# Int16 sums in seven buffers, differences on VectorE and a later load of the node rows in a two-layer graph kernel

## What is computed

```python
xn = _layernorm(x)
out = xn @ root + bias
for r in range(8):
    mask = (edge_type == r)
    sums = segment_sum(xn[src] * mask[:, None], dst, 625)
    cnt = segment_sum(mask, dst, 625)
    out = out + (sums / max(cnt, 1)[:, None]) @ weight[r]
```

## Time and profile before

| | us |
|---|---|
| median of 3 runs | 2971.97 |
| lowest and highest | 2968.42 and 2972.78 |
| the profiled execution | 2970.98 |
| its span, first to last instruction | 2969.2 |
| tallies, first to last matmul | 1832.77 to 2035.31 |
| start of the first sums of relation 0 | 2054.69 |

### The profile page before, as it was taken

The page is one execution under the profiler, slowest core; times in us unless marked ns, Lnnn a source line. Parts: engine busy times, 40 slices in busy tenths (PEclk is TensorE's granted clock), DMA queues, the critical chain, the costliest instruction groups (busy, mean ns, idle before and its releaser), DMA issues.

```text
span 2969.2 us, 39308 instructions
## 1 busy us (share of the span) xinstructions
PE 2723.3 (92%) x15859; PEld 2364.4 (80%) x15859; DVE 1805.1 (61%) x2019; ACT 1309.2 (44%) x1669; POOL 527.2 (18%) x475
## 2 busy tenths in 40 slices
PE   5989988999999999999679996789999999999988
PEld 5967778777777767776569995468999999999987
DVE  6467654778787887787635555676444444444443
ACT  3225422666766766766256665563111111112221
POOL 5776405431230000000100000343000000000000
PEclk8999999999999999999889998799999999999989
DMA  5224016999998999999441113676222221132212
GB/s 147 68 74 121 1 57 191 317 327 323 326 332 321 334 323 328 330 320 325 155 167 43 43 40 103 217 255 223 79 79 79 72 72 50 50 120 77 74 55 70
DMA packets 151178, 496.61 MB, mean 167 GB/s; under 512 B 25419, under 2 KB 38091, under 8 KB 149986
## 3 DMA queue, kind: packets, MB, share of 16 engines
q1 hardware_dynamic: 116482, 429.41, 41.4%
q0 software_dynamic: 19424, 41.25, 4.9%
q10 hardware_dynamic: 15092, 23.44, 2.5%
HBM read 422.70 MB, written 71.13 MB: 166 GB/s over the span
## 4 chain that ended last, share of the span: by engine, by line
PE 74%; DVE 10%; DMA 7%; ACT 3%; POOL 3%; issue 2%; SPq 0%; ACTq 0%; DVEq 0%; POOLq 0%
PE ps L195 73%; DMA er<-in_wd 3%; POOL lc L1419 2%; DVE es_l L220 2%; DVE T_l L220 2%; ACT es_h L682 1%; DMA scr_tl<-T_l 1%; DMA scr_adj<-acc 1%; DMA wr<-in_Wk 1%; DVE acc L216 1%; DVE x L208 0%; PE ps L1747 0%; ACT ws_h L682 0%; DVE ws_l L220 0%; PE ps L1059 0%
## 5 line engine op out<-in xcount | busy, mean ns | idle before, releaser
L220 DVE TENSOR_TENSOR es_l<-er,es_h 128x1408 fp32r<-128x1408 f32 (+1 forms) x455 | 654.1, 1446 | 196.6 <-ACT es_h L682 192.9
L682 ACT ACTIVATE es_h<-er 128x1408 fp32r<-128x1408 f32 (+1 forms) x455 | 563.8, 1242 | 260.6 <-PE ps L195 179.3
L195 PE MATMUL ps<-T_h,ws_h 128*128 128x314 f32 x1856 | 431.2, 314 | 22.1 <-DVE T_l L220 13.8
L682 ACT ACTIVATE ws_h<-wr 128x1024 fp32r<-128x1024 f32 (+1 forms) x181 | 190.8, 1054 | 553.4 <-PE ps L195 502.6
L195 PE MATMUL ps<-T_h,ws_l 128*128 128x314 f32 x1856 | 421.5, 308 | 0.0
L195 PE MATMUL ps<-T_l,ws_h 128*128 128x314 f32 x1856 | 420.7, 308 | 0.0
L195 PEld LDWEIGHTS ps<-T_h,ws_h 128*128 128x128 f32 x1856 | 311.4, 191 | 30.7 <-DVE T_l L220 16.1
L195 PEld LDWEIGHTS ps<-T_h,ws_l 128*128 128x128 f32 x1856 | 312.5, 191 | 0.0
L195 PEld LDWEIGHTS ps<-T_l,ws_h 128*128 128x128 f32 x1856 | 312.5, 190 | 0.0
L220 DVE TENSOR_TENSOR ws_l<-wr,ws_h 128x1024 fp32r<-128x1024 f32 x173 | 210.1, 1216 | 129.8 <-ACT ws_h L682 128.0
L195 PE MATMUL ps<-es_h,xe_h 128*98 128x512 f32 (+1 forms) x768 | 208.4, 379 | 10.3 <-DVE es_l L220 6.9
(11 more groups left out here) (427 smaller groups left out, 5083.7 us busy)
## 6 DMA issues: line engine op xcount, KB each, us to landing
er<-in_wg SPq DMA_DIRECT2D x128, 704.0 KB, 6.8
er<-in_wu SPq DMA_DIRECT2D x128, 704.0 KB, 5.9
er<-in_wd SPq DMA_DIRECT2D x176, 512.0 KB, 5.1
scr_adj<-acc SPq DMA_DIRECT2D x123, 314.0 KB, 2.9
wr<-in_rel SPq DMA_DIRECT2D x64, 512.0 KB, 3.5
wr<-in_Wqkv SPq DMA_DIRECT2D x24, 512.0 KB, 3.5
steps<-scr_adj POOLq DMA_DIRECT2D x7, 1570.0 KB, 8.1
wr<-in_gate SPq DMA_DIRECT2D x16, 512.0 KB, 3.5
```

What stands on the lines that cost most here:

```text
L195: return e.matmul(out, l, r, start=start, stop=stop, skip_group_check=True)
L220: return e.tensor_tensor(lo, src, hi.bitcast(F32), ALU.subtract)
L682: q.e.activation(c.hi, c.at, ACT.Copy).then_inc(*self.s("high").up(c.key))
```

## The change

- `acc`, `scr_adj` and `steps` are int16 instead of float32. `acc` has seven buffers, and `v_tally` of chunk c waits for the store of c-7. `steps` has two buffers.
- The rows by nodes are loaded by GpSimd (`p_back`): `nat_h` just before `blc` of chunk 64, `nat_l` just before that of chunk 72.
- VectorE takes the differences (`v_counts`): those of relation 0 block by block before `v_over` of relation 0, those of relation r+1 after the third `ua` of relation r. GpSimd only issues the loads (`p_steps`).

```diff
-        for i in range(4):
-            at(f"acc{i}", R3 + 20224 + i * 2528, NT)
+        for i in range(7):
+            at(f"acc{i}", R3 + 20224 + i * 1280, NT, I16)
...
-        at("steps", R3, T * NT)
+        for i in range(2):
+            at(f"steps{i}", R3 + i * 6304, T * NT, I16)
...
-        if c > 3:
-            q.wait_ge(self.landed(f"tally{c % 4}"), c - 4)
+        if c > 6:
+            q.wait_ge(self.landed(f"tally{c % 7}"), c - 7)
...
+            if c in (64, 72):
+                self.p_back(q, c == 72)
             e.tensor_scalar(m[f"blc{c % 5}"], self.iota[:, 0:128], seb[:, c, 0:1], None, ALU.is_equal).then_inc(*self.s("chunk_sources").up(c))
...
+    def p_back(self, q, i):
+        n, b = (("nh", "nat_h"), ("nl", "nat_l"))[i]
+        q.wait_ge(self.s("attention_sums"), ("out", 7, 1))
+        q.wait_ge(self.s("out_low"), 7)
+        q.wait_ge(self.landed("kept_norm"), 3)
+        for f, g in shares(TP):
+            q.e.dma_start(self.m[b][f:g, :].bitcast(F32), self.d[n][f:g, :]).then_inc(*self.landed("norm_by_nodes").up(i))
...
         for r in range(8):
+            if r == 0:
+                self.v_counts(q, 0)
             self.v_over(q, r)
...
+                if o == 2 and r < 7:
+                    self.v_counts(q, r + 1)
...
         for t in range(T):
-            e.dma_start(steps[:, t, :], self.d_adj[t * 128:(t + 1) * 128, :]).then_inc(*self.landed(f"steps{t}").up(0))
-        for t in range(T):
-            q.wait_ge(self.landed(f"steps{t}"), 0)
-            e.tensor_tensor(rows(self.counts(0), T)[:, t, 0:NT - 1], steps[:, t, 1:NT], steps[:, t, 0:NT - 1], ALU.subtract).then_inc(*self.s("counts").up((0, t), 0))
+            e.dma_start(rows(m["steps0"], T)[:, t, :], self.d_adj[t * 128:(t + 1) * 128, :]).then_inc(*self.landed(f"steps_of_block{t}").up(0))
         for r in range(1, 8):
-            q.wait_ge(self.s("counts"), r - 1)
+            if r > 1:
+                q.wait_ge(self.s("counts"), r - 2)
+            self.p_steps(q, r)
+
+    def v_counts(self, q, r):
+        m = self.m
+        steps, to = rows(m[f"steps{r % 2}"], T), rows(self.counts(r), T)
+        if r == 0:
+            self.all_stored(q)
+            for i in range(2):
+                q.e.memset(self.counts(i)[0:TP, NT - 1:T * NT:NT].bitcast(I32), 0)
+            for t in range(T):
+                q.wait_ge(self.landed(f"steps_of_block{t}"), 0)
+                tt(q.e, to[:, t, 0:NT - 1], steps[:, t, 1:NT], steps[:, t, 0:NT - 1], ALU.subtract).then_inc(*self.s("counts").up((0, t), 0))
+        else:
+            q.wait_ge(self.landed(f"steps{r % 2}"), r)
             if r > 1:
                 q.wait_ge(self.s("aggregated"), (("agg", r - 2), KD - 1))
+            tt(q.e, to[:, :, 0:NT - 1], steps[:, :, 1:NT], steps[:, :, 0:NT - 1], ALU.subtract).then_inc(*self.s("counts").up(r))
```

More of the change, by code:

```diff
@@ L11 @@
 U16 = mybir.dt.uint16
+I16 = mybir.dt.int16
 AX = mybir.AxisListType.X
@@ L189, in at @@
     def at(self, name, off, n, dt=F32):
-        assert off % 32 == 0 and off + n * (2 if dt in (BF16, U16) else 4) <= self.size, (name, off, n)
+        assert off % 32 == 0 and off + n * (2 if dt in (BF16, U16, I16) else 4) <= self.size, (name, off, n)
         return self.nc.alloc_sbuf_tensor_at(name, [128, n], dt, offset=self.base + off)[:, :]
@@ L2018, in v_tally @@
         m, ps = self.m, self.ps
-        acc, was = m[f"acc{c % 4}"], m[f"acc{(c - 1) % 4}"]
+        acc, was = m[f"acc{c % 7}"], m[f"acc{(c - 1) % 7}"]
         q.wait_ge(self.s("tallied"), c)
-        if c > 3:
-            q.wait_ge(self.landed(f"tally{c % 4}"), c - 4)
+        if c > 6:
+            q.wait_ge(self.landed(f"tally{c % 7}"), c - 7)
         for i, cut, src in self.tally_halves(c):
@@ L2081, in s_store_tallies @@
                 q.wait_ge(*self.ps.done(("tally", c), i))
-            e.dma_start(self.d_adj[bass.ds(v, 128), :], m[f"acc{c % 4}"]).then_inc(*self.landed(f"tally{c % 4}").up(c))
+            e.dma_start(self.d_adj[bass.ds(v, 128), :], m[f"acc{c % 7}"]).then_inc(*self.landed(f"tally{c % 7}").up(c))
     def t_attention(self, q):
@@ L2511, in v_mean @@
         else:
-            for i in range(4):
-                q.wait_ge(self.landed(f"tally{i}"), NCH - 1 - (NCH - 1 - i) % 4)
+            self.all_stored(q)
         tt(q.e, two(m[f"ta{k % 2}"]), ps.two(ps.group[("agg", r), k][0]), two(m["icnt"]), ALU.mult).then_inc(*ps.out((("agg", r), k)))
@@ L2577, in p_relations, with p_steps @@
             if r > 1:
                 q.wait_ge(self.s("aggregated"), (("agg", r - 2), KD - 1))
-            e.tensor_tensor(rows(self.counts(r), T)[:, :, 0:NT - 1], steps[:, :, 1:NT], steps[:, :, 0:NT - 1], ALU.subtract).then_inc(*self.s("counts").up(r))
+            tt(q.e, to[:, :, 0:NT - 1], steps[:, :, 1:NT], steps[:, :, 0:NT - 1], ALU.subtract).then_inc(*self.s("counts").up(r))
+    def p_steps(self, q, r):
+        q.e.dma_start(rows(self.m[f"steps{r % 2}"], T), self.d_adj[r * T * 128:(r + 1) * T * 128, :].rearrange("(s p) n -> p s n", p=128)).then_inc(*self.landed(f"steps{r % 2}").up(r))
@@ L2583, in t_gate, with all_stored @@
+    def all_stored(self, q):
+        for i in range(7):
+            q.wait_ge(self.landed(f"tally{i}"), NCH - 1 - (NCH - 1 - i) % 7)
     def t_gate(self, q):
```

6 lines of the change are left out of this document (2 added, 4 removed).

## The result

The changed kernel takes 2932.45 us (median of 4 runs, 2928.18 to 2935.85) where the kernel before took 2971.64 in the same comparison: a ratio of 0.9869, 95% interval 0.9852 to 0.9886. Two later comparisons of the same two kernels gave 0.9887 (0.9871 to 0.9904) and 0.9902 (0.9885 to 0.9918), so the gain is 29 to 39 us; the mean of the three ratios makes it 34. The prediction was 2935, within 2923 to 2951.

A forecast was written before the change was run, and what follows sets the result against it. The prediction took TensorE, busy 92% of the span, as the bound, with gains only where it stands, mainly behind late stores. Terms of 1.4+28.9-7+6.3+6.5=36.1 us off 2971 gave 2935 us, range 2923 to 2951.

The forecast's parts named there:

- Start: Before the first tally: ACT no longer issues four DMAs, so the first tally starts earlier; gain 1.4 us.
- Stalls on stores: Tallies, chunks 4 to 122: seven buffers and half the bytes remove VectorE's waits for stores; gain 28.9 us together.
- The rows by nodes: Tallies near chunks 66 and 74: the later bulk load stalls stores once, then near 0; loss 7 us, bounds 0 and 16.
- Rival A: Tallies: the bulk load stalls twice, a loss of 12 to 16 us for 7; 2940 to 2944 us; chance 0.17.
- Rival B: Tallies: no loss from the bulk load, as seven buffers or passing stores cover it; 2928 us; chance 0.12.
- After the last store: Between tally 122 and the first sums: differences on VectorE end with the root matmuls; gain 5.0, plus 1.3 slow clock.
- rival E: Stores wait for SP, which issues them between weight loads; half of the 28.9 us comes; 2949 us; chance 0.10.
- The relations: Relations: without GpSimd's difference beside it T_l no longer holds TensorE, six times 1.08 us; gain 6.5 us.
- C: Relations: T_l did not hold TensorE, or VectorE comes late; 6.5 shrinks to 4 or nothing; 2938 to 2942; chance 0.10.
- D: Tallies: int16 slows VectorE's tally, which then sets the pitch; 65 us of loss against 36 of gain; 3000 us; chance 0.04.
- the signs that I had named: Right if store waits fall under 8 us, tally 122 starts 20 to 26 us earlier, T_l takes 0.80 us throughout, among others.

The follow-up runs named there:

- its likes: Two runs with the kernel before unaltered up to tally 122: VectorE taking the differences, 2956.79 us; GpSimd's difference made to wait, 2957.01 us.
- the later difference: The kernel before, with GpSimd's difference for relations 1 to 7 waiting for the third block of the previous relation's product: 2957.01 us, ratio 0.9971.

## Why the prediction was right, and where it was not

The time was right, but as a sum whose two largest errors nearly cancelled: the load cost some 3 us more than I gave it, and the relations gained 2.7 more. Part of it is luck besides, since the profile that the stalls were read from had 4.5 us more of them than its likes.

*Start* (1.4): shown, 1.39, and given back when ScalarE issues the load again.

*Stalls on stores* (28.9): without the load the same stretches, 4 to 122, are 29.5 us shorter than in the profile of before, and 25 shorter than in its two likes. The sum took one profile's stalls as the kernel's, 4.5 us too many. The reason was half wrong too. I named seven buffers and half the bytes, and spoke of "nearly all that gets in its way" without saying what that is: apart from the load of the rows by nodes it is mostly the weight load on the same queue (17.0 of the 34.1 us), in which the bytes of a store have next to no part. Of int16 with four buffers I expected a loss of 5 to 12 us, and it was 24.

*The rows by nodes* (a loss of 7, between 0 and 16): 9.3 to 10.6. The mechanism held, one full stall and a second near nothing, but the first was mis-sized at "4 to 5 us" where VectorE waited 9.4. The step that failed is the length of a half, 9.5 to 10 us from 133 packets in 10 us, with the end of the crawl put 12 to 13 us behind tally 59. With a weight load and seven stores beside it the two DMAs of the half landed after 13.5 and 16.0 us, and the store issued with them after 15.9, which is 17.6 us behind tally 59. Rival A's 12 to 16 is off on the other side, and for the wrong reason: not two stalls, but one longer, though VectorE did wait a second time, 3.5 us at chunk 74. Rival B, no loss, is refuted for whole rows. The two queues in three stretches of that time, 1922 to 1927, 1927 to 1930 and, when the load had ended, 1935 to 1938 us (the first number counts the profile's packets):

```profile
q0 software_dynamic: 57, 1.17, 93.1%
```

```profile
q0 software_dynamic: 42, 0.86, 103.0%
q1 hardware_dynamic: 41, 0.05, 7.5%
```

```profile
q1 hardware_dynamic: 635, 1.00, 98.0%
q0 software_dynamic: 3, 0.00, 0.2%
```

For 5 us the stores, of which four were issued in that time, moved nothing at all. Then they moved one packet for one of the load's, but a packet of theirs has 1,256 bytes and one of the load's 20,480, so that a third of a store (41 of 128) passed in 3 us. Behind the load 635 went in 3 us. By the Trainium skill ("DMA: Bandwidth & Descriptors", Queues, rings and completion order) an engine drains a whole packet of one queue, some 9 to 17 descriptors, before it turns to the next. In the prediction I had taken that as help for the stores, and the trace of before as speaking against it. It would hold for the load's rows as well, of which an engine gets some 8 (125 over 16 engines), and the stores would stand behind all of them. The trace agrees for the first 5 us and not for the next 3, in which the two queues moved 42 and 41. No run here shows where a packet in the skill's sense ends, so that the rule behind this stays open.

*After the last store* (5.0, with 1.3 for the slow clock): 3.9. I had the differences and the root matmuls end together. They ended 2.2 us apart:

```profile
2011.79 1.03 SPq L664 DMA_DIRECT2D wr<-in_rel  x1
2013.39 2.24 SPq L2095 DMA_DIRECT2D scr_adj<-acc  x3
...
2019.96 2.80 POOL L2576 DMA_DIRECT2D steps<-scr_adj  x5 [11.34 <-DMA scr_adj<-acc]
...
2024.66 2.97 DVE L209 TENSOR_TENSOR A_h<-steps 128x627 fp32r<-128x627 int16 x4 [1.14 <-DMA steps<-scr_adj]
2025.51 0.79 ACT L2496 ACTIVATE ua<-ps,bcol 128x628 f32<-128x628 f32 x1 [6.35 <-PE ps L196]
```

SyncE put a relation's weights ahead of the last three stores, for 1.03 us, and issued the last at 2015.30, 1.4 us behind VectorE where I had 0.2; it landed in 3.8 us where I had 3.3, and the rest of the chain took about 0.2 us more than I gave it. This is rival E's mechanism, at one place and for 1 us.

*The relations* (6.5): 10.2, of which 1.0 is the slow clock at the first sums (the first period was 82.9 us, the next five 81.9), that I had booked with 1.3 at the step before. The rest, 9.2, is 6 x 1.5. I took TensorE's wait from the row of its matmuls, 1.08. The row of its weight loads stands beside it with 1.34 (in the fence above), so the matmuls' row did not hold all of it. A period before is 81.9 us and a period after 80.36: that difference, 1.5, was to be had from the trace of before. The last relation of before, beside which no difference runs, has 80.32.

The rivals C and D are refuted: T_l takes 0.80 us throughout and no wait of TensorE is left in the relations, and int16 costs nothing.

Of the signs that I had named, the time of tally 122 (22.7 us earlier), T_l and the tally's two forms came as said. VectorE's waits for stores did not: 12.9 us where I had under 8, and the second one ended 34 us behind the issue of `nat_h`, not within 25. Nor did the first sums, 2.6 us behind the end of the root matmuls where I had 2.

## What to carry to other kernels

How many buffers a stream of stores needs was set here by what stood ahead of a store or beside it in the queues, and hardly by the store's own bytes. The measure is the longest landing, against the time until a buffer is needed again: the number of buffers times the pitch, less the step that fills one and its issue (at the waits measured 1.7 to 3.2 us with four, 4.2 to 5.3 with five, 6.5 and over with seven). A bulk load beside such a stream should be cut up and spread until the longest landing is under that time; moving it whole only moved its stall. Whether the size of a piece, the length of its rows or the distance between pieces did it, these runs do not say. What a wait costs the engine that sets the pace is best taken as the difference of two periods with and without it, since each row of idle time sees only its part.

## What the runs showed of the hardware that I had not expected

The price of the collision: GpSimd's whole instruction. The longest T_l of the kernel before took 5.48 us for 0.80, and `ws_l` beside the later difference 5.48 for 1.21:

```profile
L220 DVE TENSOR_TENSOR T_l<-ta,T_h x58: 800/804/5476, 2079.9 to 2652.5; 128x628 fp32r<-128x628 f32 x58
```

The type of what is read costs VectorE nothing: 3135 elements took 3414 ns from int16, and 3415 at the most from float32. A store of half the bytes lands sooner, but by less than half. Without a bulk load and with seven buffers the float32 stores (314 KB) took 3.3 us from issue to landing at the median and the int16 ones (157 KB) 2.3; with four buffers, and the bulk load beside some of them, 2.9 to 3.0 and 2.4. It changed the kernel's time by nothing that these runs can tell, since the late stores were late by other transfers. And the two engines hold each other up in both directions: GpSimd's instruction is the longer one where VectorE's began first (5.93 us for 5.40).
